# First attention of a hybrid layer stack: which engine copies the transposed weights out of the ring of banks

## The chip, the cores and the metric

The program runs on one core of a Trainium2 chip. The metric is the device time of one execution in microseconds (us). TensorE is called PE below, its weight loads PEld, VectorE DVE, ScalarE ACT, GpSimd POOL and SyncE SP.

## The reference

Four blocks, each a residual on a layer-normalised input. `x` has 2 batches of 2048 rows of 256 numbers. Only the first block matters here:

```
def attn_a(x, Wq, Wk, Wv, Wo, bo):            # 16 heads of 64, two batches
    q, k, v = x @ Wq, x @ Wk, x @ Wv           # split into heads
    scores = q @ k.T * 64 ** -0.5 + slope[head] * (i - j)
    scores = where(i >= j, scores, -1e30)      # causal
    return softmax(scores) @ v @ Wo + bo
x = x + attn_a(layernorm(x))
x = x + ffn(layernorm(x))       # eight experts, the best two
x = x + attn_b(layernorm(x))    # hyperbolic attention
x = x + ffn(layernorm(x))
```

## The kernel before

`stage_attn_a` (from L375) computes the first attention. It makes 16 passes: 2 batches times 8 pairs of heads, each pass the same `body` on every engine (DVE from L641, ACT from L761, PE from L903). For each batch seven passes are one hardware loop and the eighth is written out, because it also prepares what follows: the eighth of the first batch (`crossing`) normalises and transposes the second batch's input, and the eighth of either batch adds the statistics for the next layer norm on DVE (`after.sums`).

A pass works through 16 tiles of 128 query rows, from the longest row (2048 keys, tile 0) to the shortest (128 keys, tile 15), in 20 steps that are staggered: in step n the scores of tile n are made (`S`), the softmax of tile n-1 runs, and the weights of tile n-2 are transposed (`T`). An `A` is a product of transposed weights with the values, in the even steps from 4 on, `O` the output projection, in the odd steps from 5 on, `V` the projection of the values (steps 0 and 1), `C` the copy of the product, and `P` the projections for the next pass (steps 16 to 19). `order()` writes this sequence down and all engines follow it in their own queues, in order.

What each engine does in a step:

- PE: for each `S`, the scores of both heads for up to 512 keys; for each `T`, up to four 128x128 transposes for head 0 and up to four for head 1, each head into one PSUM bank; the products of `A`.
- DVE: after each `S`, adds the position bias to both heads' scores and takes the row maximum (L679); at the end of the tile the negated maximum (L685); for the tile before, the reciprocal of the row sums and the scaling of the whole row (L655, L658, `invert`), for head 0 in the middle of the step and for head 1 at its end; adds the output projection to `X` (L699).
- ACT: two exponentials for the tile before, one for each head (L756), at the beginning of the step, in place over the whole row; the copies of the banks (L738).

The transposes of `T`, the values of `V` and the output projection of `O` go through a ring of three PSUM banks (4, 5 and 7). The class `Ring` numbers what passes through it. A pass has 92 such entries in the plain ring: 0 to 3 are `V`, 8 are `O`, and 80 are the two heads' halves of the `T`. I write e59 for entry 59. Entry e uses bank e mod 3, so PE may fill it only when entry e-3 has been copied out (`bank_free`). `on_dve` says for each entry which engine copies it: `O` always goes to DVE, `X` (the transposed input in the crossing pass) to ACT, and of the others every sixth goes to DVE:

```
for entry in self.entries:
    self.on_dve += [entry[0] == "O" or (entry[0] != "X" and n % 6 == 5)]
    n += entry[0] != "X"
```

In a pass these are e5, e11, e17, e23, e29, e35, e41, e47, e53, e59, e65, e71, e77 and e89, all of them `T` entries (e83 is an `O`). Eleven of the fourteen are four transposes wide (128x512), e71 is 128x384, e35 and e89 are 128x128. The copies are issued by `copy_weights`, which both engines call with their own side of the table; the DVE copies are recorded at L551 and the ACT copies at L738. Steps of interest: e4 to e11 are transposed in step 2, e12 to e19 in step 3, e29 to e36 in step 5 (behind the `O` e28), e57 to e62 in step 9 (behind the `O` e56), e77 to e80 in step 13 (behind the `O` e76), e89 and e90 in step 17.

Of the kernel before, what the change touches and what calls it, by code (L numbers as in the profile page):

```python
# [374 lines left out]
def stage_attn_a(nc, env, x, norm, after, experts, wqk, wv, wo, bo, slopes):  # L375
# [25 lines left out]
    def order(n, with_x):  # L401

        m, k = n - LAG, (n - 4) // 2
        s = [("S", i) for i in range(len(slots[n]))] if n < TB else []
        t = [("T", i) for i in range(len(groups[m]))] if 0 <= m < TB else []
        a = [("A", i) for i in range(len(parts[k]))] if n >= 4 and n % 2 == 0 else []
        seq = []
        for i in range(max(len(s), len(t), len(a), 1)):  # L410
            seq += s[i:i + 1]
            if i == 0 and n >= 5 and n % 2:
                seq += [("O", k)]
            seq += a[i:i + 1] + t[i:i + 1]
            if n < 2 and i % 2:
                seq += [("V", 2 * n + i // 2)]
        if a:
            seq += [("C", k)]
        if with_x and 0 <= n - X_STEP < NX:
            seq += [("X", n - X_STEP)]  # L420
        if n >= TB:
            seq += [("P", 2 * (n - TB)), ("P", 2 * (n - TB) + 1)]
        return seq

    class Ring:


        def __init__(self, with_x):
            self.order = [order(n, with_x) for n in range(STEPS)]
            self.entries = []  # L430
            for n, seq in enumerate(self.order):
                for what, i in seq:
                    self.entries += {"T": [("T", n - LAG, i, 0), ("T", n - LAG, i, 1)], "V": [("V", i)], "O": [("O", i)],
                                     "X": [("X", i, 0), ("X", i, 1)]}.get(what, [])
            self.place = {entry: e for e, entry in enumerate(self.entries)}
            self.on_dve, n = [], 0
            for entry in self.entries:
                self.on_dve += [entry[0] == "O" or (entry[0] != "X" and n % 6 == 5)]
                n += entry[0] != "X"
            self.tile_end = [self.place["T", n, len(groups[n]) - 1, 1] + 1 for n in range(TB)]  # L440

# [1455 lines left out]
```

## Time and profile before

| | |
|---|---|
| median of 3 runs | 5734.27 us (5729.2 to 5734.58) |
| the profiled execution | 5730.4 us, its span 5728.3 us |
| first attention | about the first 2290 us of the span |
| PE busy over the span | 4099.9 us (72%) |
| DVE busy | 4707.3 us (82%) |
| ACT busy | 4469.5 us (78%) |
| POOL busy | 1430.8 us (25%) |

The page of the profile cuts the span into 40 slices of 143 us. In the first sixteen, which are the first attention, PE is busy for nine tenths and more of nearly every slice, DVE for six or seven tenths and ACT for five. From the nineteenth slice on, the second attention, DVE and ACT stand at nine tenths and PE at five. PE's granted clock is nine tenths or more in the first seventeen slices and six or seven tenths in nearly all later ones.

How to read it: an engine's busy time is the sum of its instructions. PE's instructions overlap at their ends, so a PE row that follows another without a gap in the timeline may still have waited for up to the length of that overlap; the starts of the rows tell more than the busy time.

### The profile page before, as it was taken

What the parts mean: (1) busy time and instruction counts of PE and PEld (TensorE: products, weight loads), DVE (VectorE), ACT (ScalarE), POOL (GpSimd) and SP (SyncE); (2) the same over time, 40 slices, a digit from 0 to 9 for tenths busy, and PEclk for the clock granted to TensorE, in tenths of its full rate; (3) what the DMA queues carried; (4) which work ended last, traced back from release to release, by engine and by line L of the source; (5) the groups of instructions that cost most, each with busy time, mean ns of one, the idle gap of its engine ahead of it and who ended that gap; (6) DMA issues with size and microseconds to landing.
All of it is one profiled execution on the core that took longest, in us unless ns stands there. A gap on an engine that the chain in (4) does not pass through costs nothing. (4 is left out here: it accounts for less than half of the span.)

```text
span 5728.3 us, 68965 instructions
## 1 busy us (share of the span) xinstructions
PE 4099.9 (72%) x22020; PEld 1827.5 (32%) x22020; DVE 4707.3 (82%) x7137; ACT 4469.5 (78%) x3424; POOL 1430.8 (25%) x1258
## 2 busy tenths in 40 slices
PE   8999999999999999855555555555555555555547
PEld 4555555555555555521111111111111111111105
DVE  7666666766666666699999999999999999999966
ACT  4555555555555555579999999999999999999993
POOL 0000000000000000034444444444444444444320
PEclk9999999999999999967667766776667666776668
DMA  1000000000000000189999999999999999989881
GB/s 40 5 5 6 5 5 5 5 5 5 5 5 5 5 5 2 64 199 189 194 190 194 189 194 190 191 195 188 197 186 198 186 198 186 198 186 198 184 190 63
DMA packets 149376, 639.48 MB, mean 112 GB/s; under 512 B 32662, under 2 KB 74840, under 8 KB 79064
## 3 DMA queue, kind: packets, MB, share of 16 engines
q0 software_dynamic: 73728, 536.90, 46.8%
q1 hardware_dynamic: 75224, 97.37, 5.2%
q8 instruction: 211, 3.46, 0.3%
q14 instruction: 213, 1.74, 0.1%
HBM read 70.22 MB, written 27.13 MB: 17 GB/s over the span
## 5 line engine op out<-in xcount | busy, mean ns | idle before, releaser
L1502 DVE SCALAR_TENSOR_TENSOR b_tiles<-b_ra_rep,b_cap,psum 128x1024 f32<-128x1024 f32 x1024 | 1261.8, 1273 | 55.3 <-PE psum L1768 53.4
L1768 PE MATMUL psum<-b_qT,b_kT 126*128 126x512 bf16 x2048 | 811.5, 507 | 673.2 <-DVE b_tiles L1502 670.1
L679 DVE CUSTOM_DVE_ANT_0 a_srow<-psum,a_bias 128x512 f32<-128x512 f32 (+3 forms) x1280 | 725.7, 607 | 494.1 <-PE psum L860 491.0
L738 ACT ACTIVATE a_pT<-psum 128x512 f32<-128x512 f32 (+3 forms) x1056 | 511.9, 527 | 657.2 <-PE psum L872 656.9
L1781 PE MATMUL psum<-b_tiles,b_v_aug 128*32 128x512 f32 x2752 | 523.9, 847 | 488.7 <-ACT b_tiles L1682 488.7
L1509 DVE TENSOR_SCALAR b_tiles<-b_tiles 128x2048 f32<-128x2048 f32 x512 | 762.3, 1489 | 4.6
L872 PE MATMUL psum<-ident,a_srow 128*128 128x128 f32 x4352 | 625.6, 280 | 70.6 <-DVE a_pT L551 32.9
L756 ACT ACTIVATE a_srow<-a_srow,a_nmax 128x1536 f32<-128x1536 f32 (+15 forms) x512 | 610.4, 1197 | 23.1 <-DVE a_nmax L685 21.2
L860 PE MATMUL psum<-a_k,a_q 64*128 64x512 f32 (+3 forms) x2560 | 623.5, 572 | 0.0
L1682 ACT ACTIVATE b_tiles<-b_tiles,b_sc 128x8192 f32<-128x8192 f32 (+1 forms) x87 | 620.9, 7137 | 2.9
L1768 PEld LDWEIGHTS psum<-b_qT,b_kT 126*128 126x128 bf16 x2048 | 156.7, 110 | 1458.1 <-DVE b_tiles L1502 1093.7
L1680 ACT ACTIVATE b_tiles<-b_tiles 128x8192 f32<-128x8192 f32 (+1 forms) x87 | 605.0, 6954 | 12.5 <-DMA b_tiles<-b_tiles 11.6
L1673 ACT ACTIVATE b_tiles<-b_tiles 128x4096 f32<-128x4096 f32 x172 | 613.1, 3611 | 1.1
L1108 DVE TENSOR_TENSOR b_tiles<-b_tiles 128x2048 f32<-128x2048 f32 x252 | 589.7, 2340 | 0.0
L872 PEld LDWEIGHTS psum<-ident,a_srow 128*128 128x128 f32 x4352 | 475.0, 141 | 321.2 <-issue 151.9
L890 PE MATMUL psum<-a_pT,a_v 128*64 128x256 f32 (+1 forms) x4608 | 541.3, 374 | 14.8 <-ACT a_pT L738 10.8
L1338 POOL DMA_DIRECT2D b_tiles<-b_tiles x344 | 310.4, 1038 | 752.4 <-ACT b_tiles L1673 741.3
L1781 PE MATMUL psum<-X,b_v_aug 128*32 128x512 f32 x1344 | 259.8, 860 | 231.9 <-ACT X L1682 231.9
L658 DVE TENSOR_SCALAR a_srow<-a_srow,a_zinv 128x1536 f32<-128x1536 f32 (+15 forms) x512 | 404.9, 791 | 18.1
L890 PEld LDWEIGHTS psum<-a_pT,a_v 128*64 128x64 f32 x4608 | 311.8, 136 | 284.6 <-issue 172.3
L1108 POOL TENSOR_TENSOR b_tiles<-b_tiles 128x2048 f32<-128x2048 f32 x84 | 302.1, 3596 | 390.0 <-DVE b_tiles L1509 390.0
L1682 ACT ACTIVATE X<-X,b_sc 128x8192 f32<-128x8192 f32 x42 | 303.0, 7214 | 1.4
(222 smaller groups left out, 5262.4 us busy)
## 6 DMA issues: line engine op xcount, KB each, us to landing
b_tiles<-b_tiles POOLq DMA_DIRECT2D x344, 1024.0 KB, 13.1
X<-b_tiles POOLq DMA_DIRECT2D x168, 1024.0 KB, 13.0
b_ra_rep<-ra_scratch SPq DMA_DIRECT2D x32, 1024.0 KB, 10.2
row_scratch<-b_tiles SPq DMA_DIRECT2D x6, 2048.0 KB, 16.2
b_qk_raw<-row_scratch SPq DMA_DIRECT2D x31, 304.0 KB, 2.9
b_v_raw<-row_scratch SPq DMA_DIRECT2D x31, 136.0 KB, 8.6
X<-in_x_dram SPq DMA_DIRECT2D x8, 512.0 KB, 6.5
a_wqk<-in_wqk_dram SPq DMA_DIRECT2D x32, 128.0 KB, 2.7
```

The lines of the kernel that those rows point to most:

```text
L679: nc.vector.tensor_tensor_reduce(out=srow[:, n % ROWS, h, a:z], in0=bank(c % 2 * 2 + h, 0, z - a), in1=bias[:, h, off + a:off + z], scale= ...
L756: nc.scalar.activation(row, row, ACT.Exp, bias=nmax[:, n, h:h + 1], accum_out=zsum[:, n, h:h + 1]).then_inc(exp_done, 1)
L860: nc.tensor.matmul(bank(c % 2 * 2 + h, 0, z - a), q_sb[rows(h), tiles[n] * P:(tiles[n] + 1) * P], k_sb[rows(h), a:z], start=True, stop=Tru ...
L872: last = nc.tensor.transpose(bank(T_BANKS[e % 3], (jt - a) * P, (jt - a + 1) * P), srow[:, n % ROWS, h, jt * P:(jt + 1) * P], env.ident[:, :])
L890: last = nc.tensor.matmul(bank(6, lo, IB)[rows(h), :], v_sb[:, jt, rows(h)], pT[:, h, jt, lo:IB], start=(jt == 0), stop=(jt == 2 * ib + 1) ...
L1108: engine.tensor_tensor(y_slot(c), a, a, ALU.mult).then_inc(S["sq_" + name], 1)
L1502: nc.vector.scalar_tensor_tensor(out=a[:, s * HALF:(s + 1) * HALF], in0=ra_rep[:, j, s * HALF:(s + 1) * HALF], scalar=cap[:, j, k:k + 1], ...
L1509: nc.vector.tensor_scalar(a, a, 1.0, 1.0 + GUARD, ALU.add, ALU.max).then_inc(S["a_ready"], 1)
L1673: nc.scalar.activation(y, y, ACT.Sqrt, bias=-1.0).then_inc(S["root_done"], 1)
L1682: nc.scalar.activation(y, y, ACT.Exp, bias=col(SHIFT), scale=col(NEG_S)).then_inc(S["w_done"], 1)
L1768: last = nc.tensor.matmul(half_ps(s)[:, i * BANK:(i + 1) * BANK], kT[:, j, k * P:(k + 1) * P], qT[:, j, cs], start=True, stop=True)
L1781: last = nc.tensor.matmul(bank(4 + j)[32 * i:32 * i + 32, :], v_aug[:, j, k, :], y_slot(c)[:, i * BANK:(i + 1) * BANK], start=(k == 0), st ...
```

## The change

The table `on_dve` keeps only the `O` entries. All other entries, so also the fourteen named above, are now copied by ACT:

```
--- before.py
+++ after.py
@@ -435,7 +435,7 @@
             self.place = {entry: e for e, entry in enumerate(self.entries)}
             self.on_dve, n = [], 0
             for entry in self.entries:
-                self.on_dve += [entry[0] == "O" or (entry[0] != "X" and n % 6 == 5)]
+                self.on_dve += [entry[0] == "O"]
                 n += entry[0] != "X"
             self.tile_end = [self.place["T", n, len(groups[n]) - 1, 1] + 1 for n in range(TB)]
```

Nothing else changes: the sequence of the work on PE, the banks and the number of copies are the same, and `bank_free` and `evacuated` follow the table, so PE waits on ACT's counter where it waited on DVE's.

ACT, end of step 2 and beginning of step 3 of the first pass (`a_pT` holds the transposed weights, the 128x1792 rows are the two exponentials of tile 2):

```order
 L544 REGISTER_ALU
 L738 ACTIVATE a_pT<-psum 128x4x128
+L544 REGISTER_ALU
+L738 ACTIVATE a_pT<-psum 128x4x128
+L544 REGISTER_ALU
+L738 ACTIVATE a_pT<-psum 128x4x128
 L754 REGISTER_ALU
 L756 ACTIVATE a_srow,a_zsum<-a_srow,a_nmax 128x1792 x2
```

Step 2's eight copies are now all in ACT's queue ahead of the exponentials of tile 2, where six were; e5 takes its place behind e4, and e11 is the last.

DVE, second half of step 9 of the first pass (the reduction is the maximum of tile 9, the reciprocal belongs to tile 8):

```order
 L684 ISA
 L685 TENSOR_REDUCE a_nmax<-a_cmax 128x2
-L544 REGISTER_ALU
-L548 REGISTER_ALU
-L551 COPY a_pT<-psum 128x4x128
 L654 REGISTER_ALU
 L655 RECIPROCAL a_zinv<-a_zsum 128x1
```

The copy of e59 stood behind the scores and the maximum of tile 9 and ahead of the second reciprocal of tile 8; it is gone from DVE.

## Rows read from the trace of the kernel before

**Rows 1.** Stretches: busy us (count) of PE, PEld, DVE, ACT, POOL; PEclk; DMA share; GB/s.

```profile
453.50:594.80 141.30, 135.96 (x852) 80.75 (x851) 94.54 (x270) 77.03 (x146) 0.00 (x0) 1.00 0.02 6
2430.00:5450.00 3020.00, 1638.50 (x7134) 358.70 (x7132) 2893.49 (x2224) 2974.62 (x785) 1361.85 (x1190) 0.69 0.91 192
```

**Rows 2.** DVE's bias for the next pass, two per pass, 400 to 1200 us: duration ns, starts.

```profile
L629 DVE TENSOR_SCALAR a_bias<-a_ahead,a_slope x12: 1280/1282/1287, 452.2 to 1159.9; 128x2048 f32<-128x2048 f32 x12
```

**Rows 3.** PE's waits in all 16 passes (50 to 2290 us): us, times, longest.

```profile
PE psum L872 <- DVE a_pT L551: 32.9, 32, 1.6
...
PE psum L872 <- ACT a_pT L738: 17.1, 16, 1.2
...
PE psum L872 <- DVE a_srow L658: 16.5, 31, 0.8
...
PE psum L890 <- DVE a_pT L551: 3.2, 4, 1.6
```

**Rows 4.** ACT's waits, 50 to 2290 us.

```profile
ACT a_pT L738 <- PE psum L872: 656.9, 496, 3.4
```

**Rows 5.** Groups of copies, wide form, 400 to 2000 us: busy us, mean ns.

```profile
L738 ACT ACTIVATE a_pT<-psum 128x512 f32<-128x512 f32 x511 | 281.9, 593 | 321.8 <-PE psum L872 321.8
...
L551 DVE COPY a_pT<-psum 128x512 f32<-128x512 f32 x125 | 86.1, 688 | 44.3 <-PE psum L872 43.8
```

**Rows 6.** Groups by line, one pass (172 to 313 us).

```profile
L551 DVE COPY a_pT<-psum 128x512 f32<-128x512 f32 (+2 forms) x14 | 8.7, 622 | 4.0 <-PE psum L872 3.9
```

**Rows 7.** Step 9, timeline: start us, length us, what, [idle before <-releaser].

```profile
552.27 1.20 PE L872 MATMUL psum<-ident,a_srow 128*128 128x128 f32 x9
...
554.53 0.33 PE L872 MATMUL psum<-ident,a_srow 128*128 128x128 f32 x1 [1.06 <-DVE a_pT L551]
...
553.40 0.77 ACT L738 ACTIVATE a_pT<-psum 128x512 f32<-128x512 f32 x2 [0.84 <-PE psum L872]
...
553.79 0.69 DVE L551 COPY a_pT<-psum 128x512 f32<-128x512 f32 x1
```

**Rows 8.** Step 13, timeline.

```profile
575.62 1.46 PE L872 MATMUL psum<-ident,a_srow 128*128 128x128 f32 x9
...
577.94 0.33 PE L872 MATMUL psum<-ident,a_srow 128*128 128x128 f32 x1 [0.86 <-DVE a_pT L551]
...
576.69 0.77 ACT L738 ACTIVATE a_pT<-psum 128x512 f32<-128x512 f32 x2 [0.77 <-PE psum L872]
...
576.00 0.69 DVE L699 TENSOR_TENSOR X<-psum,X 128x512 f32<-128x512 f32 x1
...
577.20 0.68 DVE L551 COPY a_pT<-psum 128x512 f32<-128x512 f32 x1
```

**Rows 9.** Steps 2 and 3, timeline.

```profile
484.60 1.07 ACT L738 ACTIVATE a_pT<-psum 128x512 f32<-128x512 f32 x2
...
485.24 0.66 PE L872 MATMUL psum<-ident,a_srow 128*128 128x128 f32 x4 [1.06 <-ACT a_pT L738]
...
488.54 1.09 PE L872 MATMUL psum<-ident,a_srow 128*128 128x128 f32 x8
...
489.23 0.60 ACT L738 ACTIVATE a_pT<-psum 128x512 f32<-128x512 f32 x1 [0.57 <-PE psum L872]
...
489.85 1.79 ACT L756 ACTIVATE a_srow<-a_srow,a_nmax 128x1792 f32<-128x1792 f32 x1
...
491.98 0.65 PE L872 MATMUL psum<-ident,a_srow 128*128 128x128 f32 x4 [0.70 <-DVE a_srow L658]
...
493.41 2.04 ACT L738 ACTIVATE a_pT<-psum 128x512 f32<-128x512 f32 x4
...
493.62 1.09 PE L872 MATMUL psum<-ident,a_srow 128*128 128x128 f32 x8
```

**Rows 10.** Step 5, timeline.

```profile
515.99 0.60 ACT L738 ACTIVATE a_pT<-psum 128x512 f32<-128x512 f32 x1
...
516.14 1.09 PE L872 MATMUL psum<-ident,a_srow 128*128 128x128 f32 x8
```

More of the change, by code:

```diff
@@ L437, in __init__ @@
             for entry in self.entries:
-                self.on_dve += [entry[0] == "O" or (entry[0] != "X" and n % 6 == 5)]
+                self.on_dve += [entry[0] == "O"]
                 n += entry[0] != "X"
```

## The prediction

> **What bounds the kernel now.** I read the stretches first. In one pass of the first attention PE is busy 136.0 of 141.3 us, DVE 94.5 and ACT 77.0, and PE's granted clock is 1.00, its 2.4 GHz level [rows 1]. The second attention, by far the longest stage, stands on DVE and ACT, and nothing in it is touched; so the change is worth what it does to PE's idle time in the first attention, 16 passes. That a pass lasts 141.3 us is seen from DVE's bias: twelve records, six pairs, so five periods between the first pair and the last, (1159.9 - 1.2 - 452.2) / 5 [rows 2]. Fourteen of the sixteen passes are alike; the last of each batch carries more DVE work.
>
> Then the waits of PE. What it waited for over the 16 passes is a short list [rows 3]: 32.9 + 3.2 = 36.1 us ended by a DVE copy of transposed weights, 17.1 us by an ACT copy, 16.5 us by DVE's scaling of a row. DVE makes 14 such copies in a pass [rows 6], ACT the other 66 of 80, so the larger wait belongs to the much smaller number of copies. The reader should look for where: in a steady pass only two waits are ended by a DVE copy, 1.06 us in step 9 [rows 7] and 0.86 us in step 13 [rows 8]. Together 1.92 us.
>
> Last the timelines of these places. In step 9, PE begins the pairs at 552.27: four transposes of e59, four of e60, one of e61. e62 needs e59's bank. DVE takes e59 up at 553.79 only, because the scores of tile 9 and their maximum are ahead of it in its queue, and PE goes on at 554.53. ACT meanwhile has been idle for 0.84 us before it takes e60 at 553.40 [rows 7]. Step 13 is the same with e77 and e80: DVE first adds an output projection (576.00) and scales a row, copies at 577.20, PE goes on at 577.94, and ACT had been idle for 0.77 us before 576.69 [rows 8].
>
> **The change, part by part.** Per pass DVE loses 8.7 us of copies [rows 6]. ACT gains eleven wide copies at 593 ns instead of 688 [rows 5] and three small ones, about 7.6 us, and goes from 77.0 to about 85 of 141.3. Neither is near its limit, and no DMA, bank or matmul is added; what counts is the order in ACT's queue. Three figures are needed. A first half of a pair is ready for its copy 0.69 us after the pair began (489.23 - 488.54, ACT was waiting) [rows 9]. The second half is ready 553.40 - 552.27 = 1.13 after, so 0.44 later [rows 7]. A copy that starts on ACT lets PE go on 485.24 - 484.60 = 0.64 us later, and two copies in a row start 0.48 apart (1.07 for two, less 0.59 for one) [rows 9].
>
> *Step 9.* e59 is ready at 552.27 + 0.69 = 552.96, ACT is idle then, PE may write e62 at 553.60 instead of 554.53: 0.93 us gained.
>
> *Step 13.* e77 is ready at 575.62 + 0.69 = 576.31, ACT is idle, e80 can start at 576.95 instead of 577.94: 0.99 gained. The wait that would be next is e79's, for the bank that DVE's addition frees at 576.00 + 0.69 = 576.69, and that is earlier.
>
> *Step 2 to 3.* Here the change costs. ACT's last copy of step 2 was e10 at 489.23, with the exponentials of tile 2 right behind it at 489.85; e11 was DVE's [rows 9]. Now e11 is ready at 489.67, is started at 489.71, and the exponentials begin at 490.19, 0.34 late. They are two of 1.79 us, and the copies of step 3 begin behind them: 493.75 instead of 493.41. PE needs the first of these, e12, for e15: that went at 493.62 + 0.44 = 494.06, just when e12's bank came free (493.41 + 0.64 = 494.05), and will now go at 494.39. What DVE gains there is no use: without e11's copy it scales the row for e13 some 0.60 us earlier, and PE's wait of 0.70 at 491.98 nearly goes, but PE then arrives earlier at e15 and stands there. So 0.34 us lost, and the wait is renamed from DVE's scaling to ACT's copy.
>
> *Step 5.* e29 now starts on ACT at 515.99, where e30 did, behind the second exponential. e32 needs its bank at 516.14 + 0.44 = 516.58, it is free at 516.63 [rows 10]: 0.05 lost.
>
> *The other ten.* e5 goes behind e4 at 485.08 and is done at 485.72, while e8 comes at 486.88. The rest of them lie in steps where `A` keeps PE longer; ACT stands idle before its copies for 656.9 us in all, 496 times, 1.3 us on average [rows 4], and that is the cover. If it were gone, each would cost up to 0.48. I take 0.
>
> *A steady pass:* -0.93 - 0.99 + 0.34 + 0.05 = -1.53 us, and 14 of them -21.4. *The last pass of each batch:* of the 36.1 us of waits on DVE copies, 14 x 1.92 = 26.9 are in the steady passes, so 9.2 in these two, where the statistics of the next layer norm are ahead of the copy in DVE's queue. ACT has none of that; I take them as gone and charge 2 x 0.39: -8.4. **Sum: -29.8 us**, from the profiled execution's 5730.4 to 5700.6. The median of the runs lies 3.9 us above that execution, so I forecast 5704.5, rounded 5705. This kernel's measurement can tell about 0.2% (11.5 us) from no change.
>
> The unseen quantity is ACT's lateness with more copies in its queue. From below: it costs nothing anywhere, and DVE's lead of 0.60 in step 3 is kept too, -1.92 - 0.60 = -2.52 a steady pass, 35.3 in 14, with 9.2 and 1.2 in the other two 45.7 us, 5688.6. From above: every wide copy shifts PE by 0.48. I take the value near the first end, since in the timelines ACT waits for PE at most copies.
>
> The parallel drain speaks against this change. A pair split between DVE and ACT is emptied by both at once, a pair on ACT 0.48 us one after the other [rows 9]. The Trainium skill (PSUM — Partial Sum Buffer, Specifications (TRN2)) says that ScalarE and VectorE can read PSUM in parallel at full bandwidth while they don't collide in a bank; by that alone one engine for the whole ring is the worse choice at all eleven wide copies. The trace agrees that both can work at once, but shows that DVE came late to its half in steps 9 and 13.
>
> **The rivals.** *A: ACT's queue becomes the bound (slower).* A wide copy that ACT must make behind two exponentials or behind the other half shifts PE by 0.48. With four such in a pass (4 x 0.48 = 1.92) the gain of a steady pass is gone; beyond that it decides. With the seven wide copies of steps 2 to 7 (e5, e11, e17, e23, e29, e41, e47): 3.36 - 1.92 = +1.44 a pass, 14 times +20.2, the two others 6.7 - 9.2 = -2.5: +18, 5752. For it: e11 does just that, and e15 has no slack. Against: ACT's idle time [rows 4]. This is also what the skill's rule on parallel access would do here.
>
> *B: ACT isn't free in time (no change).* In steps 9 and 13 it takes e59 and e77 only where it took e60 and e78 (0.44 and 0.38 later), and the shift of step 3 comes twice: -1.92 + 0.82 + 0.68 + 0.05 = -0.37 a pass, -5.2 in 14; the two others 2 x 1.55 - 9.2 = -6.1; together -11.3: 5723. Against: the idle 0.84 and 0.77 us [rows 7, 8].
>
> *C: nothing is lost on ACT*, the lower end above: 5689. Against: the equal numbers 494.05 and 494.06 in step 3. That the change doesn't do what it says is excluded, since the copies are seen moved in both queues.
>
> **How the numbers follow.** Forecast 73 in 100, with an own range of 5698 to 5714; A 8, B 12, C 7. Faster by over 0.2% is the forecast and C: 0.80. Within 0.2% is B, at its edge, with what lies between B and A: 0.12. Slower is A: 0.08. The range takes in the forecast and B with a little on either side, 5694 to 5728, and leaves out A and C, 15 in 100.
>
> **What would show it.** A steady pass of 139.8 us in the spacing of DVE's bias. Among PE's waits none ended by a DVE copy; that on a row's scaling in step 3 about 0.1 instead of 0.70, and a new one of some 0.8 to 1.1 us at the second half of step 3's second pair, ended by ACT. No row for e62 and e80. The exponential of tile 2 about 0.34 us later against the start of its step. I'd be wrong if waits on ACT's copies grow in steps 2 to 7 beyond 1.92 us a pass (A), or if e62 and e80 still wait (B).

## The result and the profile after

| | before | changed kernel |
|---|---|---|
| median of 4 runs, us | 5731.8 (5729.2 to 5734.58) | 5695.22 (5694.48 to 5696.99) |
| profiled execution: span, us | 5728.3 | 5693.5 |
| first rows of the feed-forward block on PE, us | 2293.11 | 2259.20 |

The kernel before has a fourth run here, so its median is 5731.8 and not the 5734.27 of the table above. The ratio is 0.9937 with a 95% interval of 0.9923 to 0.9951: faster by 0.6%, 36.6 us in the medians and 34.8 us in the spans. Of these 34.8 us, 33.9 are there when the first attention ends.

The first lines of the page show the copies on the other engine: DVE has 224 instructions and 120.7 us less, ACT 224 more and 85.4 us more, 5.3 us a pass (the prediction had reckoned with about 7.6).

```profile
PE 4098.7 (72%) x22020; PEld 1821.6 (32%) x22020; DVE 4586.6 (81%) x6913; ACT 4554.9 (80%) x3648; POOL 1429.7 (25%) x1258
```

The waits of PE in the 16 passes of the changed kernel, 50 to 2290 us: in total, times, longest. They answer to [rows 3].

```profile
PE psum L872 <- ACT a_pT L738: 36.0, 46, 1.2
PE psum L890 <- ACT a_pT L738: 10.8, 15, 0.7
...
PE psum L901 <- ACT a_oT L738: 1.3, 2, 0.8
PE psum L890 <- DVE X L699: 0.7, 1, 0.7
PE psum L872 <- DVE a_srow L658: 0.3, 1, 0.3
```

No wait is ended by a DVE copy; 36.1 us of them are gone. The waits of transposes on ACT's copies are up from 17.1 us in 16 to 36.0 us in 46, and those on DVE's scaling down from 16.5 us in 31 to 0.3 in one. 16 waits of step 3 and, at e90 in step 17, 14 of 0.39 us have changed their name from DVE's scaling to ACT's copy.

The length of a pass is the spacing of DVE's pairs of bias rows. First the kernel before, then the changed one; the four rows of each are the pair at the end of the first pass, the one ahead of the crossing pass, the one behind it, and the last. (`x2` and 2.48 us are the pair.)

```profile
171.57 2.48 DVE L629 TENSOR_SCALAR a_bias<-a_ahead,a_slope 128x2048 f32<-128x2048 f32 x2
...
1013.60 2.48 DVE L629 TENSOR_SCALAR a_bias<-a_ahead,a_slope 128x2048 f32<-128x2048 f32 x2
...
1158.68 2.48 DVE L629 TENSOR_SCALAR a_bias<-a_ahead,a_slope 128x2048 f32<-128x2048 f32 x2
...
2141.21 2.48 DVE L629 TENSOR_SCALAR a_bias<-a_ahead,a_slope 128x2048 f32<-128x2048 f32 x2
```

```profile
169.46 2.48 DVE L629 TENSOR_SCALAR a_bias<-a_ahead,a_slope 128x2048 f32<-128x2048 f32 x2
...
1001.21 2.48 DVE L629 TENSOR_SCALAR a_bias<-a_ahead,a_slope 128x2048 f32<-128x2048 f32 x2
...
1142.97 2.48 DVE L629 TENSOR_SCALAR a_bias<-a_ahead,a_slope 128x2048 f32<-128x2048 f32 x2
...
2113.68 2.49 DVE L629 TENSOR_SCALAR a_bias<-a_ahead,a_slope 128x2048 f32<-128x2048 f32 x2
```

Between the first two rows lie six steady passes: (1013.60 - 171.57) / 6 = 140.34 us before, (1001.21 - 169.46) / 6 = 138.62 after, 1.72 less. The crossing pass went from 145.08 to 141.76, 3.3 less. From the last pair to the feed-forward block it is 151.90 and 145.52, 6.4 less. So the 33.9 us are 24.2 in the fourteen steady passes and 9.7 in the two others. In the last of these the kernel before waited four times for a DVE copy: at e62, at the product of step 12, at e80, and at the product behind e89.

```profile
2244.03 0.33 PE L872 MATMUL psum<-ident,a_srow 128*128 128x128 f32 x1 [1.63 <-DVE a_pT L551]
2258.55 1.95 PE L890 MATMUL psum<-a_pT,a_v 128*64 128x256 f32 x16 [0.61 <-DVE a_pT L551]
2268.70 0.33 PE L872 MATMUL psum<-ident,a_srow 128*128 128x128 f32 x1 [1.64 <-DVE a_pT L551]
2282.42 1.55 PE L890 MATMUL psum<-a_pT,a_v 128*64 128x256 f32 x8 [1.64 <-DVE a_pT L551]
```

The spacing of the pairs also shows that the pass length read ahead of the experiments, 141.3 us, was wrong: the twelve records of [rows 2] reach across the crossing pass.

The steady pass of the changed kernel in the view of the stretches, with the columns of [rows 1]: PE has its 135.0 us, at the same clock, in less time; DVE and ACT now carry nearly the same.

```profile
459.30:597.96 138.66, 135.03 (x850) 79.86 (x849) 85.96 (x254) 82.30 (x160) 0.00 (x0) 1.00 0.02 6
```

Step 9 of a steady pass in the changed kernel (PE and ACT), against [rows 7]:

```profile
547.05 1.67 PE L872 MATMUL psum<-ident,a_srow 128*128 128x128 f32 x10
548.65 1.13 PE L860 MATMUL psum<-a_k,a_q 64*128 64x512 f32 x4
...
547.74 1.43 ACT L738 ACTIVATE a_pT<-psum 128x512 f32<-128x512 f32 x4 [0.40 <-PE psum L872]
```

The ten transposes of e59 to e62 now stand in one row without a gap. ACT takes e59 up at 547.74, 0.69 us after PE began. The scores of the next tile follow 1.60 us after the pair; before, they followed at 554.79, 2.52 us after 552.27 (next fence). Step 13 is the same, 1.57 instead of 2.58 us:

```profile
569.37 1.61 PE L872 MATMUL psum<-ident,a_srow 128*128 128x128 f32 x10
570.94 0.70 PE L860 MATMUL psum<-a_k,a_q 64*128 64x256 f32 x4
...
570.00 1.43 ACT L738 ACTIVATE a_pT<-psum 128x512 f32<-128x512 f32 x4 [0.33 <-PE psum L872]
```

PE's scores behind the same transposes in the kernel before, in steps 3, 9 and 13, and the product of step 8:

```profile
494.65 1.13 PE L860 MATMUL psum<-a_k,a_q 64*128 64x512 f32 x4
...
539.32 1.95 PE L890 MATMUL psum<-a_pT,a_v 128*64 128x256 f32 x16
...
554.79 1.13 PE L860 MATMUL psum<-a_k,a_q 64*128 64x512 f32 x4
...
578.20 0.70 PE L860 MATMUL psum<-a_k,a_q 64*128 64x256 f32 x4
```

Steps 2 and 3 of the changed kernel, against [rows 9]. PE first, then ACT, then DVE:

```profile
485.10 1.31 PE L872 MATMUL psum<-ident,a_srow 128*128 128x128 f32 x8
...
488.87 0.66 PE L872 MATMUL psum<-ident,a_srow 128*128 128x128 f32 x4 [0.81 <-ACT a_pT L738]
489.45 1.13 PE L860 MATMUL psum<-a_k,a_q 64*128 64x512 f32 x4
...
483.71 1.09 ACT L738 ACTIVATE a_pT<-psum 128x512 f32<-128x512 f32 x2 [0.57 <-PE psum L872]
484.68 1.79 ACT L756 ACTIVATE a_srow<-a_srow,a_nmax 128x1792 f32<-128x1792 f32 x1
...
488.22 2.05 ACT L738 ACTIVATE a_pT<-psum 128x512 f32<-128x512 f32 x4
...
484.41 1.22 DVE L658 TENSOR_SCALAR a_srow<-a_srow,a_zinv 128x1920 f32<-128x1920 f32 x1
```

All times of this pass are 5.53 us earlier than in the pass of [rows 9], up to here. ACT copies e10 and e11 in a row (483.71, two) and begins the exponentials at 484.68, where 489.85 - 5.53 = 484.32 would be unchanged: 0.36 late. PE's wait for DVE's scaling is no longer listed, but a part is left: the row of eight at 485.10 takes 1.31 us, where the same eight take 1.09 elsewhere (488.54 in [rows 9]), and its second half needs the row that DVE finishes at 484.41 + 1.22 = 485.63. So about 0.2 us of it remain, hidden inside a row (0.1 was forecast). PE then reaches e15 early, and waits there for ACT's copy of e12 (488.22 + 0.64 = 488.86). The next scores start at 489.45 instead of 489.12, 0.33 late.

### The profile page after: what moved, and what is told of

It reads as the page before. It is cut to its first block and busy times, and to the rows that moved or that the text cites. A ratio compares the mean times of both kernels' runs of the same rounds, so it can differ in the third digit from the quotient of the medians.

```text
span 5693.5 us, 68825 instructions
## 1 busy us (share of the span) xinstructions
PE 4098.7 (72%) x22020; PEld 1821.6 (32%) x22020; DVE 4586.6 (81%) x6913; ACT 4554.9 (80%) x3648; POOL 1429.7 (25%) x1258
## 5 line engine op out<-in xcount | busy, mean ns | idle before, releaser
L738 ACT ACTIVATE a_pT<-psum 128x512 f32<-128x512 f32 (+3 forms) x1280 | 603.4, 533 | 558.7 <-PE psum L872 558.5
L890 PE MATMUL psum<-a_pT,a_v 128*64 128x256 f32 (+1 forms) x4608 | 540.6, 374 | 11.5 <-ACT a_pT L738 10.8
L890 PEld LDWEIGHTS psum<-a_pT,a_v 128*64 128x64 f32 x4608 | 306.6, 136 | 284.0 <-issue 167.5
```

The source lines that it names most:

```text
L890: last = nc.tensor.matmul(bank(6, lo, IB)[rows(h), :], v_sb[:, jt, rows(h)], pT[:, h, jt, lo:IB], start=(jt == 0), stop=(jt == 2 * ib + 1) ...
```

## The experiments

The runs are named e1 to e10, like entries of the ring. Below, "run e4" is always a run, and a bare e4 or "the copy of e4" an entry.

Each changes only the condition in `Ring`, in this form, with another tuple; the entries in it are DVE's:

```
-                self.on_dve += [entry[0] == "O" or (entry[0] != "X" and n % 6 == 5)]
+                self.on_dve += [entry[0] == "O" or (entry[0] != "X" and n in (4, 12))]
```

Two theories stood against each other. *Places:* the gain is the two waits of e62 and e80, in which DVE came late to a bank, and everything else is a few tenths. *Load:* the gain comes from less work on DVE and from the shorter copy on ACT, and goes with the copied time that is moved. Each time is given beside that of the kernel before on the same chip; "pass" is the steady pass of the first loop (the first batch), from the bias rows.

| run | copies on DVE besides `O` | us | before, us | ratio, 95% interval | pass, us |
|---|---|---|---|---|---|
| before | every sixth, 14 | | | | 140.34 |
| change | none | 5695.2 | 5731.8 | 0.9937 (0.9923 to 0.9951) | 138.62 |
| e1 | 14 without e59, e77 | 5695.3 | 5730.7 | 0.9939 (0.9923 to 0.9956) | 138.40 |
| e2 | e59, e77 | 5730.1 | 5730.7 | 1.0000 (0.9990 to 1.0009) | 140.57 |
| e3 | 14 without e11 | 5735.7 | 5730.7 | 1.0007 (0.9998 to 1.0017) | 140.69 |
| e4 | entry e11 | 5690.9 | 5730.7 | 0.9932 (0.9916 to 0.9949) | 138.42 |
| e5 | entries e4, e12 | 5661.3 | 5728.4 | 0.9884 (0.9867 to 0.9900) | 136.33 |
| e6 | entry e4 | 5675.4 | 5728.4 | 0.9908 (0.9892 to 0.9925) | 137.48 |
| e7 | entry e12 | 5679.6 | 5728.4 | 0.9915 (0.9898 to 0.9931) | 137.74 |
| e8 | entries e4, e11, e12 | 5671.5 | 5728.4 | 0.9900 (0.9883 to 0.9916) | 136.99 |
| e9 | 14 without e5, e17, e23, e41, e53, e65 | 5731.1 | 5729.3 | 1.0000 (0.9991 to 1.0009) | 140.35 |
| e10 | 14 without e47, e71 | 5729.5 | 5729.3 | 0.9997 (0.9988 to 1.0006) | 140.49 |

**Run e1: two copies moved.**

```
n in (5, 11, 17, 23, 29, 35, 41, 47, 53, 65, 71, 89)
```

> Only e59 and e77 go to ACT; the other twelve copies stay on DVE as before. Theory 'places' (the gain of the change is the wait of e62 and of e80 for a bank that DVE empties late, everything else is small): a steady pass loses 0.92 + 1.01 = 1.93 us, 14 passes 27.0; the last pass of each batch, where these two waits show 1.63 and 1.05 to 1.64 us, loses about 6 together: 33 us less than before, about 5699, close to the change itself. Theory 'load' (DVE is relieved and ACT's copies are shorter, so the gain goes with the copied time moved, 2 x 0.69 of 8.7 us): 16 in 100 of 36.6, so 6 us less, about 5726.

5695.3 us, the time of the full change, and 4 us less than expected. The waits of PE in this run, 50 to 2290 us; all three are as in the kernel before, to 0.1 us [rows 3], and of the 32 waits on DVE's copies with 32.9 us none is left:

```profile
PE psum L872 <- ACT a_pT L738: 17.1, 16, 1.2
PE psum L872 <- DVE a_srow L658: 16.4, 31, 0.8
...
PE psum L890 <- DVE a_pT L551: 3.2, 4, 1.6
```

So two of fourteen copies make the whole gain; load is refuted.

**Run e2: the other twelve moved.**

```
n in (59, 77)
```

> The other way round: twelve copies go to ACT, e59 and e77 stay on DVE. Places: a steady pass gains 0.33 (e11) + 0.06 (e29) and loses 0.09 (e47) + 0.10 (e71), +0.20 us; 14 passes +2.8; the last passes lose about 1.5 with e71 and e89; together +1, about 5733, no change. Load: 84 in 100 of 36.6, 31 us less, about 5701.

No change in the time, +0.23 us in the pass where 0.20 was expected. The two last passes are 0.9 and 1.4 us shorter, which makes up for most of that. DVE is relieved of 84 in 100 of the copied time and nothing comes of it.

**Run e9: six whose next user comes late.**

```
n in (11, 29, 35, 47, 59, 71, 77, 89)
```

> Only e5, e17, e23, e41, e53 and e65 go to ACT, six wide copies whose next user comes late on both engines; e11, e29, e35, e47, e59, e71, e77 and e89 stay on DVE. Places: the start of every group of matmuls in a steady pass stays where it was, to 0.02 us; no difference, 5731. Load: 4.1 of 8.7 us moved, 17 us less, 5714.

The pass is 140.35 against 140.34, the ratio 1.0000, and PE's waits are those of before, to 0.2 us:

```profile
PE psum L872 <- DVE a_pT L551: 32.9, 32, 1.6
PE psum L872 <- ACT a_pT L738: 17.1, 16, 1.2
PE psum L872 <- DVE a_srow L658: 16.3, 31, 0.7
```

Moving nearly half of the copied time, with 4 us less on DVE in each pass, is worth nothing where PE doesn't need the bank soon. One thing in this trace is not as before: from the last bias pair to the feed-forward block it is 155.18 us against 151.90. Most of that stands in two rows of sixteen products of the last pass, 2.80 and 3.17 us long where they took 1.95, and no wait on a copy is listed there; the median doesn't show it. So the length of that pass in a single execution can differ by 3 us without a cause in the copies.

**Run e3: e11 alone moved.**

```
n in (5, 17, 23, 29, 35, 41, 47, 53, 59, 65, 71, 77, 89)
```

> Only e11 goes to ACT. Places, with the cost of step 3 as forecast: the exponentials of tile 2 begin about 0.34 us late, PE's wait of 0.70 on DVE's scaling in step 3 goes and one on ACT's copy of e12 comes: +0.33 us a pass, +5 us in 16, about 5737. Load: 3 us less, about 5729.

The pass is 0.35 us longer, and the feed-forward block starts 5.2 us later than before (2298.26 against 2293.11). The time alone doesn't settle it (its interval includes 1), the pass does. The waits of PE show the exchange: 16 more waits on an ACT copy, 16 fewer on the scaling.

```profile
PE psum L872 <- ACT a_pT L738: 29.9, 32, 1.2
...
PE psum L872 <- DVE a_srow L658: 5.8, 15, 0.4
```

**Run e4: e11 kept.**

```
n in (11,)
```

> All copies on ACT but e11, which stays on DVE. Places: against the change 0.33 us less a pass, 5 in 16, about 5690; PE's wait on DVE's scaling in step 3 is back at about 0.70 and the wait of 0.80 on ACT's copy in step 3 is gone. Load: 3 us more than the change, about 5698.

5690.9, where 5690 was expected: 4.3 us less than the change, or 3.2 by what each is below its own kernel before; the feed-forward block starts 5.0 us earlier (2254.22). The wait on DVE's scaling is back in step 3 and the one on the copy of e12 is gone, as expected. Over the steps, PE's starts behind e15 are 0.33 us earlier than in the change. The pass of the first loop is only 0.20 shorter because 0.16 is lost again in step 13, where ACT takes 1.56 us for the four copies instead of 1.43; in the second loop, with the same instructions, it is 138.26 against 138.6 to 138.7.

**Run e10: e47 and e71 moved.**

```
n in (5, 11, 17, 23, 29, 35, 41, 53, 59, 65, 77, 89)
```

> Only e47 and e71 go to ACT. These are the last DVE copies before a product with the values begins (A of steps 8 and 12), which waits for all copies of its tiles. Places: no wait is recorded there in a steady pass, because it lies inside the overlap of PE's rows, but the starts say 0.09 and 0.10 us: 0.19 a pass, 2.7 in 14, and 0.61 us of recorded wait in each last pass: 4 us less, 5727, best seen in the starts. Load: 1.25 of 8.7 us moved, 5 us less; the time can't tell the two apart here, the starts can: load would spread it.

The time shows nothing of the 4 us expected, as the interval reaches 5 us to either side. PE's starts are 0.09 us earlier behind step 8 and 0.10 behind step 12, as expected; the second loop's pass is 140.11 instead of 140.31. But in the first loop the pass got longer, 140.49. All of it is in step 9: PE waits 1.42 us for e59's copy where it waited 1.06. DVE in step 9, first the kernel before, then this run:

```profile
553.60 0.16 DVE L685 TENSOR_REDUCE a_nmax<-a_cmax 128x2 f32<-128x4 f32 x1
```

```profile
553.53 0.16 DVE L685 TENSOR_REDUCE a_nmax<-a_cmax 128x2 f32<-128x4 f32 x1
554.07 0.69 DVE L551 COPY a_pT<-psum 128x512 f32<-128x512 f32 x1 [0.38 <-issue]
```

Behind the same reduction the copy came 0.19 us later in the kernel before (553.79) [rows 7] and 0.54 us here, with nothing in the profile to wait for. By the pass lengths it happens in every pass of the first loop and in none of the second. What causes it stays open.

**Where the remaining waits are: runs e5 to e8.** In the change two large waits of a steady pass are left in steps 2 and 3, at e7 (1.06 us) and at e15 (0.81), each for ACT's first copy of the step (e4, e12) behind two exponentials. In both places DVE has just read the step's scores. A third wait, of 0.73 us at a product near the end of the pass (L890 for ACT's copies, 10.8 us in 15), is the same in every run; none tried to remove it.

**Run e5: e4 and e12 on DVE.**

```
n in (4, 12)
```

> All copies on ACT but e4 and e12, which DVE makes. These are the first copies of steps 2 and 3, the ones for which PE waits behind ACT's two exponentials in the change (1.06 us at e7, 0.80 at e15). Theory 'first copy' (ACT is late only with the first bank of a step; DVE has just read the scores of that step and is free): both waits go, about 1.13 + 0.93 us a pass against the change, 16 passes 33 us, about 5662. Rival 'shifted' (the waits move to the next bank, e8 for e5 and e16 for e13, or to DVE's scaling of tile 1): half or less of it, 5680 to 5695.

5661.3 us, 5662 expected. Steps 2 and 3 on PE (starts, lengths), then DVE's two copies, and the exponentials that ACT is busy with at that time:

```profile
470.62 1.09 PE L872 MATMUL psum<-ident,a_srow 128*128 128x128 f32 x8
...
476.44 1.32 PE L872 MATMUL psum<-ident,a_srow 128*128 128x128 f32 x8
477.69 1.13 PE L860 MATMUL psum<-a_k,a_q 64*128 64x512 f32 x4
478.75 1.09 PE L872 MATMUL psum<-ident,a_srow 128*128 128x128 f32 x8
479.77 1.13 PE L860 MATMUL psum<-a_k,a_q 64*128 64x512 f32 x4
...
469.98 0.69 DVE L551 COPY a_pT<-psum 128x512 f32<-128x512 f32 x1
478.11 0.69 DVE L551 COPY a_pT<-psum 128x512 f32<-128x512 f32 x1
...
469.82 1.89 ACT L756 ACTIVATE a_srow<-a_srow,a_nmax 128x1920 f32<-128x1920 f32 x1
477.80 1.78 ACT L756 ACTIVATE a_srow<-a_srow,a_nmax 128x1792 f32<-128x1792 f32 x1
```

The pairs e6, e7 (470.62) and e14, e15 (478.75) are rows of eight now; both waits are gone. In the first loop none has come in their place. In the second loop PE waits 0.30 us for DVE's scaling in step 3, and the pass is 136.75 there against 138.6 to 138.7 in the change: 1.9 us less, not 2.3. This is the best of the versions run, 1.2% below the kernel before and 0.5 to 0.6% below the change.

**Runs e6 and e7: one of the two.**

```
n in (4,)
n in (12,)
```

> All copies on ACT but e4. First copy: the wait at e7 (1.06 us) goes, 1.13 us a pass, 18 us, about 5677; the wait at e15 stays at 0.80 or grows a little, because PE reaches step 3 earlier while ACT doesn't. If it grows by the whole of it, nothing is left: 5695.

> All copies on ACT but e12. First copy: the wait at e15 (0.80 us, 0.93 from start to start) goes, 15 us, about 5680; the wait at e7 stays 1.06. Shifted: PE waits at e16 for e13 instead, 5690 to 5695.

5675.4 (5677 expected) and 5679.6 (5680). Against the change the pass is 1.14 and 0.88 us shorter, and 2.29 with both. The missing 0.27 is in step 13, where ACT's four copies take 1.56 us in runs e6 and e7 (as in run e4) and 1.43 in run e5 and the change. By PE's starts behind step 3 the gains are 1.28, 1.03 and 2.29: they add up. In the first loop the wait at e15 stayed 0.80 in run e6: it doesn't grow when e7's goes. ACT's queue moves forward together with PE, since the exponentials of tile 2 begin behind the copies of step 2, and these follow PE's transposes: counted from the bias pair they begin at 36.68 us in run e6 and at 37.96 in the change, 1.28 earlier. In the second loop the wait at e15 is 0.44, with one of 0.38 on DVE's scaling ahead of it; the change has 0.84 there.

**Run e8: e11 on DVE as well.**

```
n in (4, 11, 12)
```

> All copies on ACT but e4, e11 and e12. If the exponentials of tile 2 beginning 0.34 us late still cost anything when e12 is off ACT's queue, this is faster than the same kernel with e11 on ACT by up to 5 us (about 5657); if not, it is slower, because e11's copy then again stands ahead of DVE's scaling of tile 1, for which e13 waited 0.70 us: up to +10 us (about 5672).

5671.5, 10 us slower than run e5, and PE waits for DVE's scaling again (2.4 us in 8 in run e5):

```profile
PE psum L872 <- DVE a_srow L658: 13.6, 17, 1.0
```

So whether e11 belongs on DVE depends on the copies around it: with e4 and e12 on ACT it is worth 3 to 4 us there (run e4), with both on DVE it costs 10. That it is e12 that decides, for which PE waits longer at e15 when the exponentials are late, is my reading; no run has e11 on DVE with only one of the two.

## Why the prediction was right

It forecast 29.8 us less and 5705; measured were 36.6 us in the medians (34.8 in the spans) and 5695. The sign, the places and the waits by name came out. The size came out less well: 5695.2 lies 1 us inside the range of 5694 to 5728 and outside the 5698 to 5714 given for the forecast itself, and it is nearer to rival C's 5689 than to 5705. The time alone wouldn't have told the two apart; the trace does, by the 0.33 us that are lost in step 3.

Of the 9.3 us between 5704.5 and 5695.2, the sum missed 5.3. The other 4.0 are the step from the profiled execution to the median: 3.9 us had been added for it from the three runs of the kernel before, and the changed kernel doesn't have it (5695.29 profiled, 5695.22 median). In the starts of PE's groups, the same steady pass before and after, the terms are:

| term | forecast, us | measured, us |
|---|---|---|
| step 9, e59 | -0.93 | -0.92 |
| step 13, e77 | -0.99 | -1.01 |
| step 3, e11 | +0.34 | +0.33 |
| step 5, e29 | +0.05 | +0.06 |
| step 8, e47 | 0 | -0.09 |
| step 12, e71 | 0 | -0.10 |
| steady pass | -1.53 | -1.72 |
| 14 steady passes | -21.4 | -24.2 |
| the last pass of each batch, together | -8.4 | -9.7 |

- *The other ten at 0* was mis-sized by two small terms. The copies of e47 and e71 held up the first product of steps 8 and 12 by 0.1 us each. PE's rows overlap at their ends, so a wait of that length isn't listed; only the starts show it (the row at 539.32 follows scores at 538.17, and scores of this width take 1.06 from start to start elsewhere, so 539.23 was due). Run e10 confirms both in the starts. They are worth 2.7 us in fourteen passes. Run e9 confirms the zero for the six others it moved.
- *The last passes* were 1.3 us better, nearly all of it in the second batch. The crossing pass has listed waits on DVE copies of 1.63, 0.61, 1.05 and 0.30 us; less the 0.39 charged, about 3.2, and it gained 3.3. The last pass of the second batch has 5.5 as shown above, less 0.39: 5.1, and it gained 6.4. With e59 and e77 alone moved (run e1) it gained 4.95, where their two waits are 3.27. What makes the rest is open. These are single executions, and run e9 shows 3.3 us of difference in the same place.
- A pass of 141.3 us was a wrong reading, as shown above: the right one is 140.34. The sum didn't rest on it, but the forecast of 139.8 for the pass would have had to be 138.8; measured 138.62.
- 0.9 us of the span's difference lies behind the first attention, and 1.8 us more is the difference between the medians and the profiled executions; the kernel before alone spread from 5725 to 5735 over all its runs. I have no cause for these in the copies.
- *Rival A* had four wide copies as its point of decision. One of them (e11) and a trace of another (e29) shifted PE. Run e3 shows that its mechanism is real at that one place, run e2 that all twelve together cost 0.23 us a pass. *Rival B* fell with e62 and e80: ACT took e59 up 0.69 us after the pair began, as its idle time had said. *Rival C* fell with step 3.
- The rule on parallel access in the Trainium skill (PSUM — Partial Sum Buffer, Specifications (TRN2)) is not what decided. The trace of before agrees with it: in step 9 DVE's copy (553.79, 0.69 us) runs beside ACT's (553.40, 0.77 us for two) and takes no longer than DVE's wide copies do on average, 688 ns [rows 5, 7]. But only at e11 and e29 did giving up the second engine cost PE anything in a steady pass, 0.33 and 0.06 us. Nor does run e5 owe its 30 to 34 us against the change to parallel draining: both DVE copies lie inside an exponential of ACT, when ACT drains nothing. The Trainium skill (Perfetto Trace Analysis, Optimizing Scalar/DVE Operations) also says that where Scalar or Vector aren't saturated but cause bubbles elsewhere, breaking up instructions may let work complete sooner. The trace agrees with the first half: two exponentials of 1.89 and two of 1.79 us, on an ACT busy 82.3 of 138.7 us, held the banks of e4 and e12. Here the copies were given to the other engine; splitting the exponentials wasn't tried.

## What to carry to other kernels

In a ring of banks that two engines empty in order, look for what is ahead of a copy in its engine's queue and when the producer needs the bank again, and place each copy by that; a rule by count (every sixth) mixes copies worth a microsecond with copies worth nothing. The first copy behind long instructions of one engine is the one to give to the other. After a wait has been moved, try the neighbouring copies again: DVE's copy of e11 changed from a gain of 3 to 4 us to a loss of 10 when e4 and e12 moved to DVE.

## What was not expected

- The same instructions can run with an extra gap in one loop and without it in another. DVE's 0.35 us in step 9 of run e10 is there in the first loop and missing in the second, ACT's 0.13 us in step 13 of run e4 likewise, run e5's pass is 136.33 in the first loop and 136.75 in the second, and passes of the changed kernel in the second loop are 138.62 or 138.71. The profile names no releaser. Differences of 0.1 to 0.4 us a pass between versions should therefore be read from the starts of single steps, not from the pass length.
- Taking one of two successive waits away didn't lengthen the other: in the first loop the wait at e15 is 0.81 us with the wait at e7 (the change) and 0.80 without it (run e6).
